# Convolution, attention and experts over 16 images: the next image's start inside the expert layer, combine weights by DMA, and the score tiles of a pair apart

## The chip, the cores and the metric

One core of a Trainium2 chip runs the whole program. The metric is the time on the device in microseconds (us), lower is better. The core has TensorE (PE, matmuls; PEld is its weight load), VectorE (DVE), ScalarE (ACT), GpSimd (POOL) and SyncE (SP, which issues the DMA transfers here). They run side by side and wait for each other through semaphores. Matmuls write into PSUM, which has 8 banks of 128 x 512 values.

## The reference

Sixteen images of 256 channels by 1024 pixels go through three layers. Cut to what is computed:

```
q, k, v = 1x1 convolutions of x to 32 channels
x = conv1x1(softmax(q @ k) @ v, Wo) * gamma + x          # 32 x 32 channel attention
t = tokens(x)                                            # 1024 tokens of 256
n = layernorm(t)
a1 = softmax(q1 @ k1 / s); a2 = softmax(q2 @ k2 / s)     # 8 heads of 32, over 1024 keys
o  = (a1 - lam * a2) @ v                                 # two softmaxes a head
t  = t + groupnorm(o) @ out_w.T + out_b
n = layernorm(t)
probs = softmax(n @ router); combine = the two largest of 8, else 0
y = shared(n) + sum over e of combine[:, e] * ((silu(n @ Wg[e]) * (n @ Wu[e])) @ Wd[e])
out = t + y
```

## The kernel before, in words

One loop over the 16 images ("batches"). The order of the work on every engine is written out by hand, and each engine keeps to it.

**Projection and first scores.** `layer_norm(0)` turns the normalised tokens back to channels. Four query and key projections follow (`proj`), written as three matmuls a product (a value split in a high and a low part, `split_mm`, L853). ACT takes the high part of each into `stage` (L385, L387), DVE the low part (L609), and SP copies both to `stack`. ACT waits for `y_out[1]`, the store of the image before, ahead of the first of these, since both use `stage`.

**Attention.** There are 16 units (8 heads, two softmaxes), each with 8 key tiles, taken as 4 pairs of tiles: 64 pairs. Of each key tile PE makes the transposed scores of 128 keys by 1024 queries as two matmuls (L1033, to PSUM banks 4 and 5, one half each), ACT takes the exponential of each half into `probs` (L411), and PE multiplies with the values (`weighted`, L985). A column of sums (`add_up`, L992) follows in three pairs of four. There is only one PSUM bank for each half, so the matmul of a tile's half waits until ACT has taken the same half of the tile before.

The maximum that the softmax subtracts is found 12 tiles ahead: PE makes the plain scores of 128 queries by 1024 keys (`score`, L964), DVE reduces them (L614). The eight columns of a unit are then turned by a transpose (`turn`, L970), which DVE takes out in a high and a low part (L623, L624) and SP puts into `stack`. Scores, turns and projections share a ring of two PSUM slots (four banks): item n waits for DVE to have freed item n - 2 (`ring_free`). `ring_order()` lists which items stand beside which pair (`BESIDE`): two scores a pair, the turn in pair 2 of a unit, and the four projections of the second head group in pairs (5, 1), (5, 2), (5, 3) and (6, 0). The last six pairs have no score beside them.

**Expert layer.** After the output projection (L1057) and the second layer norm come the router, its choice of two experts (a chain of small DVE steps, L768 to L786), and 18 steps (2 halves of the tokens, the shared expert and 8 experts). Step i on PE: gate and up (12 matmuls, L853), then a matmul (L1117) with a selecting column that spreads row e of the combine weights `comb_t` over all 128 partitions, then `down(i - 2)` (6 matmuls, L1087). `comb_t` is split in two parts by ACT (L463) and DVE (L805). On ACT: tanh (L470) and the high part of the hidden values (L455). On DVE: three products (L818, L826, L827; the last one with the spread weights out of PSUM), then the low part of the step before (L791). `down(i)` waits for the low part of step i.

**The next image.** Its convolution is spread over steps 9 to 11 (`conv_q`, `conv_scores`, `conv_wo`). `conv_last` (L897), the transposes to tokens (L917), the statistics and the normalisation stand behind the last step, between `down(15)` and the first projection, with `down(16)` and `down(17)` among them.

## Time and profile before

| | |
|---|---|
| median of 3 runs | 6543.28 us (6539.59 to 6547.5) |
| profiled execution | 6535.96 us, its span 6533.1 us |
| busy, share of the span | PE 93%, DVE 72%, ACT 47%, POOL 47% |
| granted TensorE clock, mean | 0.97 |
| chain that ended last, by engine | PE 82%, DVE 10%, ACT 3%, issue 3%, DMA 1% |
| one image | about 403 us |

The span is what lies between the first and the last instruction; the profiled execution's own time is 3 us above it. A clock of 1.00 is 2.4 GHz, one of 0.50 is 1.2 GHz. A busy time counts a matmul from its start to its end, though the next one starts before that: back to back, 512 columns start every 0.23 us. A start is therefore more use than a duration here.

### The profile page before, as it was taken

How to read it: one execution, taken by the hardware profiler on the slowest of the kernel's cores; microseconds unless marked ns; L12 is line 12 of the kernel's file. 1: busy time of each engine (PE TensorE's matmuls, PEld its weight loads, DVE VectorE, ACT ScalarE, POOL GpSimd, SP SyncE). 2: the span in 40 equal slices, each digit the busy share in tenths (PEclk: the TensorE clock that was granted, in tenths of full speed). 3: DMA queues.
4: the chain of work that ended last, by engine and by line, in shares of the span. 5: the costliest groups of instructions: out<-in, count | busy, mean ns of one | idle time of the engine just before them, and what ended most of it. 6: DMA issues, size and time to landing. Idle time of an engine off the chain costs nothing.

```text
span 6533.1 us, 125913 instructions
## 1 busy us (share of the span) xinstructions
PE 6063.3 (93%) x41498; PEld 3899.9 (60%) x41498; DVE 4700.7 (72%) x6535; ACT 3089.8 (47%) x5470; POOL 3092.9 (47%) x1382
## 2 busy tenths in 40 slices
PE   6999999899999999999999999999999999999998
PEld 4565565655656566565665656556565565655656
DVE  5767777676776767767677676776767767677676
ACT  4535445354453544535445354453544535355353
POOL 3706437074470734707347073471725617256271
PEclk9999999999999999999999999999999999999999
DMA  2202122121221212212022120221202212021120
GB/s 77 49 27 52 32 47 45 31 51 28 48 45 30 53 29 45 45 29 58 25 48 48 28 54 24 50 47 28 59 19 51 47 32 55 18 55 43 37 54 17
DMA packets 111217, 271.38 MB, mean 42 GB/s; under 512 B 34000, under 2 KB 56656, under 8 KB 102096
## 3 DMA queue, kind: packets, MB, share of 16 engines
q1 hardware_dynamic: 110544, 262.73, 17.4%
q8 instruction: 384, 6.29, 0.4%
q14 instruction: 289, 2.37, 0.1%
HBM read 23.38 MB, written 16.78 MB: 6 GB/s over the span
## 4 chain that ended last, share of the span: by engine, by line
PE 82%; DVE 10%; ACT 3%; issue 3%; DMA 1%; SPq 0%; DVEq 0%; ACTq 0%
PE psum L1033 19%; PE psum L853 17%; PE psum L985 15%; PE psum L964 14%; PE psum L1087 5%; PE psum L992 5%; DVE minus_max L614 2%; PE psum L1057 2%; PE psum L1012 1%; DVE small L550 1%; ACT probs L411 1%; PE psum L1117 1%; DVE max_rows L623 1%; DVE max_rows L624 1%; DMA stack<-stage 1%
## 5 line engine op out<-in xcount | busy, mean ns | idle before, releaser
L329 POOL TENSOR_TENSOR prob_sums<-probs 128x1024 f32<-128x1024 f32 x752 | 1795.2, 2387 | 3207.9 <-ACT probs L411 2923.4
L411 ACT ACTIVATE probs<-psum 128x512 f32<-128x512 f32 x4096 | 2222.9, 595 | 1419.9 <-PE psum L1033 1408.0
L614 DVE TENSOR_REDUCE minus_max<-psum 128x1 f32<-128x1024 f32 x2048 | 2422.4, 1209 | 398.6 <-PE psum L964 391.7
L1033 PE MATMUL psum<-stack 98*128 98x512 f32 x4096 | 1479.5, 438 | 43.9 <-ACT probs L411 41.7
L964 PE MATMUL psum<-stack 96*128 96x512 f32 x4096 | 1241.3, 412 | 106.0 <-DVE max_rows L624 64.9
L329 POOL TENSOR_TENSOR prob_sums<-prob_sums,probs 128x1024 f32<-128x1024 f32 x512 | 1220.2, 2383 | 101.5 <-ACT probs L411 62.6
L1033 PEld LDWEIGHTS psum<-stack 98*128 98x128 f32 x4096 | 704.9, 190 | 737.3 <-ACT probs L411 480.2
L985 PE MATMUL psum<-probs,v_tokens 128*32 128x256 f32 x16384 | 1112.2, 388 | 0.0
L964 PEld LDWEIGHTS psum<-stack 96*128 96x128 f32 x4096 | 721.5, 191 | 409.2 <-DVE max_rows L624 171.2
L853 PE MATMUL psum<-act_hi,w_hi 128*128 128x512 f32 x1728 | 713.7, 413 | 62.0 <-DVE minus_max L614 48.3
L985 PEld LDWEIGHTS psum<-probs,v_tokens 128*32 128x32 f32 x16384 | 429.4, 109 | 465.8 <-issue 288.9
L853 PE MATMUL psum<-act_lo,w_hi 128*128 128x512 f32 x1728 | 697.2, 403 | 0.0
L853 PE MATMUL psum<-act_hi,w_lo 128*128 128x512 f32 x1728 | 694.7, 402 | 0.0
L470 ACT ACTIVATE stage<-psum 128x512 f32<-128x512 f32 x288 | 172.6, 599 | 897.1 <-PE psum L1117 813.1
L635 DVE RECIPROCAL recip_sum<-psum 128x128 f32<-128x128 f32 x512 | 472.7, 931 | 118.7 <-PE psum L992 115.4
L818 DVE SCALAR_TENSOR_TENSOR stage<-stage,psum 128x512 f32<-128x512 f32 x288 | 197.6, 686 | 431.6 <-ACT stage L470 431.6
L992 PE MATMUL psum<-prob_sums,ones 128*32 128x256 f32 x6016 | 462.2, 379 | 0.0
L853 PEld LDWEIGHTS psum<-act_hi,w_hi 128*128 128x128 f32 x1728 | 334.8, 194 | 174.5 <-DVE minus_max L614 75.8
L1087 PE MATMUL psum<-stack,w_hi 128*128 128x512 f32 x1152 | 414.8, 401 | 6.0 <-DVE small L564 6.0
L853 PEld LDWEIGHTS psum<-act_lo,w_hi 128*128 128x128 f32 x1728 | 334.8, 194 | 78.1
L853 PEld LDWEIGHTS psum<-act_hi,w_lo 128*128 128x128 f32 x1728 | 335.7, 194 | 73.7
L992 PEld LDWEIGHTS psum<-prob_sums,ones 128*32 128x32 f32 x6016 | 195.6, 110 | 129.0
(141 smaller groups left out, 4744.7 us busy)
## 6 DMA issues: line engine op xcount, KB each, us to landing
stack<-stage SPq DMA_DIRECT2D x1024, 128.0 KB, 3.0
stack<-stage SPq DMA_DIRECT2D x256, 256.0 KB, 3.1
x_tile<-x_dram SPq DMA_DIRECT2D x17, 1024.0 KB, 4.8
x_tile<-o_head SPq DMA_DIRECT2D x512, 32.0 KB, 1.8
stack<-max_rows SPq DMA_DIRECT2D x512, 4.0 KB
y_dram<-residual SPq DMA_DIRECT2D x16, 512.0 KB, 2.8
y_dram<-stage SPq DMA_DIRECT2D x16, 512.0 KB, 3.7
stage<-w_split_dram SPq DMA_DIRECT2D x1, 3848.0 KB, 12.5
```

Source lines behind the costliest of these rows:

```text
L329: nc.gpsimd.tensor_tensor(total, first, probs[:, k % NP, :], ALU.add).then_inc(sum_pool, 1)
L411: nc.scalar.activation(probs[:, k % NP, half * HALF:(half + 1) * HALF], ps[:, 4 + half, :], ACT.Exp).then_inc(p_ready, 1)
L470: nc.scalar.activation(th[:, i % 2, :], ps[:, 2 + 3 * (i % 2), :], ACT.Tanh, scale=0.5).then_inc(f_th, 1)
L614: v.tensor_reduce(nm[:, u % 2, q:q + 1], flat_in, AX.X, ALU.max, negate=True).then_inc(ring_free, 1)
L635: v.reciprocal(rec[:, cols], ps[:, 6 + u % 2, CQ + cols.start:CQ + cols.stop]).then_inc(step, 1)
L818: link(v.scalar_tensor_tensor(gu, th[:, i % 2, :], 1.0, ps[:, bank, :], ALU.add, ALU.mult))
L853: ins = mm(dst, wt[:, w + kt * wn[0]:w + kt * wn[0] + wn[1]], xx[:, kt, act_cols], start=(first and n == 0), stop=(last and n == 3 * CT - 1))
L964: last = mm(slot[:, half, :], stack[0:AUX, s, 0, q * P:(q + 1) * P], stack[0:AUX, s, 1, half * HALF:(half + 1) * HALF], start=True, stop=True)
L985: last = mm(ps[HD * c:HD * c + HD, bank, 0:CQ], vt[:, kt, HD * h:HD * h + HD], probs[:, k % NP, c * CQ:(c + 1) * CQ], start=(kt == 0), sto ...
L992: ins = mm(ps[HD * c:HD * c + HD, 6 + u % 2, CQ:2 * CQ], ones[:, :], tile[:, c * CQ:(c + 1) * CQ], start=False, stop=last, skip_group_chec ...
L1033: mm(ps[:, 4 + half, :], stack[0:KS, s, 1, kt * P:(kt + 1) * P], stack[0:KS, s, 0, half * HALF:(half + 1) * HALF], start=True, stop=True). ...
L1087: last = mm(ps[:, t, :], wt[:, col:col + P], hx[:, i % 2, :], start=(e == 0 and n == 0), stop=(e == NE - 1 and n == 2))
```

## The change

Three parts, made together.

1. **The next image inside the expert layer.** `conv_q`, `conv_scores`, `conv_wo` move to steps 0, 1 and 3, `conv_last` to steps 4 and 5, the transposes to tokens to steps 6 and 8, statistics and normalisation to steps 7 to 13, half of the transposes back to step 12, the other half behind the gate and up of step 17. They use the two PSUM banks `SPARE = (4, 7)`; tokens are copied out of PSUM by ACT and normalised in place there. The sum goes to `x_tile` and is copied to `residual` later. The first half of projection 0 stands ahead of `down(17)`.
2. **Combine weights spread by transfers.** L1117 and the split of `comb_t` go. ACT copies the weights to SBUF, SP stores them in DRAM (32 KB) and, when that has landed, reads each expert's row back to all 128 partitions: 8 transfers of 256 KB a half, 16 an image. DVE's third product reads them from SBUF and waits for the transfer.
3. **The score tiles of a pair apart.** Of the two scores beside a pair one stays between the pair's two key tiles, the other one goes behind the pair's `weighted` and `add_up`, with the projection. The turn goes behind the second key tile. ACT does the projection's high part a pair later.

```
-                        for item in BESIDE.get((u, pair), []):      # DVE
+                        items = BESIDE[u, pair]
+                        for item in [it for it in items if it[0] == "turn" or it == items[0]]:
                             ring_step(item)
...
-                            if kt % 2 == 0:                          # PE
-                                for item in BESIDE[u, pair]:
+                            for item in BESIDE[u, pair][:1] if kt % 2 == 0 else []:
+                                if item[0] == "score":
                                     ring_step(item)
+                        for item in BESIDE[u, pair]:
+                            if item[0] == "turn":
+                                ring_step(item)
...
                         weighted(*divmod(k - 1, NT))
                         for late in ones_after(u, pair):
                             add_up(*late)
+                        for item in BESIDE[u, pair][1:]:
+                            if item[0] != "turn":
+                                ring_step(item)
...
-                        v.tensor_tensor(hid[:, i % 2, :], guu, ps[:, bank + 2, :], ALU.mult).then_inc(f_hid, 1)
-                    if i:
+                        dve.wait_ge(cb_in[e - 1], (b * NH + half + 1) * 16)
+                        v.tensor_tensor(hid[:, i % 2, :], guu, comb_bc[e - 1], ALU.mult).then_inc(f_hid, 1)
+                    if 0 < i < NH * NE - 1:
                         hidden_lo(i - 1)
...
+                for i in range(NH * E):                              # SP
+                    half, n = divmod(i, E)
+                    if half:
+                        sp.wait_ge(f_hid, b * NH * NE + n + 2)
+                    elif n == 0:
+                        sp.wait_ge(cb_row, b + 1)
+                        sp.dma_start(comb_rows, comb_t).then_inc(cb_out, 16)
+                        sp.wait_ge(cb_out, b * 16 + 16)
+                    sp.dma_start(comb_bc[n], comb_rows[n:n + 1, half * HALF:(half + 1) * HALF]
+                                 .broadcast_to([P, HALF])).then_inc(cb_in[n], 16)
...
-                    if e:                                            # PE, expert step i
-                        last = mm(ps[:, bank + 2, :], wh[:, W_SEL + e - 1:W_SEL + e].broadcast_to([P, P]), comb_t[:, cols],
-                                  start=True, stop=True)
-                    last.then_inc(f_full, 1)
...
+                        if i == 0 and part == 0:
+                            turn_logits()
+                            conv_q(b + 1)
+                    last.then_inc(f_full, 1)
                     if i == 1:
+                        conv_scores(b + 1)
...
+                    if i == 3:
                         conv_wo(b + 1)
-                    if i >= 2:
+                    if i in (4, 5):
+                        conv_last(b + 1, i - 4)
+                    if i in (TOKENS_AT, TOKENS_AT + 2):
+                        first_tokens(b + 1, i > TOKENS_AT)
+                    if i == TOKENS_AT + 6:
+                        first_back(b + 1, 0)
+                    if i == NH * NE - 1:
+                        first_back(b + 1, 1)
+                    if i >= 2 and i < NH * NE - 1:
                         down(i - 2)
-
+                down(NH * NE - 3)
+                down(NH * NE - 2)
                 pe.wait_ge(f_hid, b * NH * NE + NH * NE - 1)
-                for k in range(3):
-                    conv_last(k)
-                pe.wait_ge(f_hid, b * NH * NE + NH * NE)
-                conv_last(3)
-                tokens(b + 1, 0)
-                down(NH * NE - 2)
-
-                pe.wait_ge(t_var, b * 2 + 3)
+                first_projection(b + 1, 0)
                 down(NH * NE - 1)
```

In the next fences a row is one instruction, or several equal ones (x2), with its line and what it writes and reads; register and semaphore instructions stand among them.

PE inside attention, one plain pair before: the two halves of a key tile (L1033), four score matmuls (L964), the second key tile, the values (L985), the sums (L992).

```order
212 L1033 MATMUL psum<-stack 128x512
213 L1032 REGISTER_ALU
214 L1033 MATMUL psum<-stack 128x512
215 L948 REGISTER_ALU
216 L964 MATMUL psum<-stack 128x512 x2
217 L948 REGISTER_ALU
218 L964 MATMUL psum<-stack 128x512 x2
219 L1032 REGISTER_ALU
220 L1033 MATMUL psum<-stack 128x512
221 L1032 REGISTER_ALU
222 L1033 MATMUL psum<-stack 128x512
223 L985 MATMUL psum<-probs,v_tokens 32x256 x8
```

PE at a like place now (L1185 is the key tile, L1116 the score, L1137 the values, L1144 the sums):

```order
178 L1116 MATMUL psum<-stack 128x512 x2
179 L1184 REGISTER_ALU
180 L1185 MATMUL psum<-stack 128x512
181 L1184 REGISTER_ALU
182 L1185 MATMUL psum<-stack 128x512
183 L1098 REGISTER_ALU
184 L1116 MATMUL psum<-stack 128x512 x2
185 L1184 REGISTER_ALU
186 L1185 MATMUL psum<-stack 128x512
187 L1184 REGISTER_ALU
188 L1185 MATMUL psum<-stack 128x512
189 L1137 MATMUL psum<-probs,v_tokens 32x256 x8
```

Two score matmuls stand between the key tiles, where four stood; the other two stand ahead of the pair.

PE at the end of the expert layer before, behind `down(15)`: the last convolution, the transposes to tokens, then the last two `down`.

```order
1561 L1125 REGISTER_ALU
1562 L897 MATMUL psum<-stage 128x512 x3
1563 L1128 REGISTER_ALU
1564 L897 MATMUL psum<-stage 128x512
1565 L915 ISA
1566 L917 MATMUL psum<-w_full,residual 128x128 x8
1567 L915 REGISTER_ALU
1568 L917 MATMUL psum<-w_full,residual 128x128 x8
1569 L1087 MATMUL psum<-stack,w_hi 128x512
```

PE there now, between the gate and up of step 17 and `down(15)` (L1246):

```order
1548 L1039 REGISTER_ALU
1549 L1042 ISA
1550 L1045 MATMUL psum<-w_full,stage 128x128 x4
1551 L1042 REGISTER_ALU
1552 L1045 MATMUL psum<-w_full,stage 128x128 x4
1553 L1246 MATMUL psum<-stack,w_hi 128x512
```

Only the second half of the transposes back is left there. DVE in steps 1 and 2 now (L935, L943 and L945 are the three products, L898 the low part of the step before):

```order
588 L935 SCALAR_TENSOR_TENSOR probs<-probs,psum 128x512
589 L619 REGISTER_ALU
590 L943 TENSOR_TENSOR probs<-probs,psum 128x512
591 L619 REGISTER_ALU
592 L944 REGISTER_ALU
593 L945 TENSOR_TENSOR probs<-probs,prob_sums 128x512
594 L898 TENSOR_TENSOR stack<-probs,stack 128x512
```

The wait for the transfer stands at 592, and the low part that `down(0)` needs (594) behind it.

## Rows read from the trace of the kernel before

**Rows 1.** Who waited for whom on PE: us in total, times, longest

```profile
PE psum L964 <- DVE max_rows L624: 64.9, 213, 0.4
PE psum L853 <- DVE minus_max L614: 48.3, 64, 0.9
```

**Rows 2.** Timeline of PE, a plain pair: start, us, then idle before

```profile
2221.97 0.84 PE L1033 MATMUL psum<-stack 98*128 98x512 f32 x2
2222.66 1.09 PE L964 MATMUL psum<-stack 96*128 96x512 f32 x4
2223.58 0.63 PE L1033 MATMUL psum<-stack 98*128 98x512 f32 x2
2224.14 1.07 PE L985 MATMUL psum<-probs,v_tokens 128*32 128x256 f32 x16
...
2225.57 0.50 PE L1033 MATMUL psum<-stack 98*128 98x512 f32 x1
```

**Rows 3.** Timeline of ACT, the exponentials of the second key tile of that pair

```profile
2224.01 1.08 ACT L411 ACTIVATE probs<-psum 128x512 f32<-128x512 f32 x2 [0.42 <-PE psum L1033]
```

**Rows 4.** Timeline of PE, a pair of the last unit, with no score beside it

```profile
2346.97 0.73 PE L1033 MATMUL psum<-stack 98*128 98x512 f32 x2
2348.15 0.99 PE L1033 MATMUL psum<-stack 98*128 98x512 f32 x2 [0.45 <-ACT probs L411]
2349.07 1.07 PE L985 MATMUL psum<-probs,v_tokens 128*32 128x256 f32 x16
...
2350.50 0.50 PE L1033 MATMUL psum<-stack 98*128 98x512 f32 x1
```

**Rows 5.** Timeline of PE, start of the pair behind a turn pair

```profile
2229.76 0.50 PE L1033 MATMUL psum<-stack 98*128 98x512 f32 x1
```

**Rows 6.** Groups of instructions: taking a projection out of PSUM, a hidden product, busy and mean ns

```profile
L609 DVE SCALAR_TENSOR_TENSOR stage<-psum,w_full,stage 128x1024 fp32r<-128x1024 f32 x64 | 82.1, 1284 | 136.8 <-ACT stage L387 136.8
L387 ACT ACTIVATE stage<-psum,w_full 128x1024 fp32r<-128x1024 f32 x64 | 71.3, 1115 | 200.6 <-PE psum L853 200.6
L827 DVE TENSOR_TENSOR stage<-stage,psum 128x512 f32<-128x512 f32 x256 | 175.7, 686 | 8.9
```

**Rows 7.** One image in stretches: us, then PE, PEld, DVE, ACT, POOL busy, PEclk, DMA

```profile
2388.68:2410.68 22.00, 18.34 (x80) 14.33 (x80) 13.59 (x31) 6.16 (x10) 0.00 (x0) 0.92 0.02 5
2410.68:2470.87 60.19, 60.02 (x273) 47.71 (x272) 36.44 (x59) 14.88 (x28) 0.00 (x0) 1.00 0.03 10
2470.87:2485.80 14.93, 14.64 (x56) 10.18 (x54) 12.68 (x31) 4.07 (x7) 0.00 (x0) 0.89 0.00 1
2485.80:2504.76 18.96, 15.15 (x66) 11.75 (x65) 8.63 (x13) 7.66 (x11) 0.00 (x0) 0.91 0.32 80
2519.07:2762.84 243.77, 233.49 (x1921) 133.07 (x1919) 187.00 (x211) 141.71 (x258) 191.30 (x86) 0.99 0.22 48
```

**Rows 8.** The same for attention of the image before

```profile
2113.00:2359.37 246.37, 236.11 (x1921) 133.93 (x1919) 187.19 (x211) 141.70 (x258) 191.33 (x86) 0.98 0.21 47
```

**Rows 9.** Timeline of all engines, the logits' turn, then the combine weights

```profile
2390.17 0.33 PE L1071 MATMUL psum<-w_full,stage 128*128 128x128 f32 x1 [1.32 <-DVE stage L765]
...
2397.68 1.01 ACT L463 ACTIVATE stack<-psum 8x1024 fp32r<-8x1024 f32 x1 [3.05 <-PE psum L1110]
...
2399.99 0.50 PE L1117 MATMUL psum<-stack,w_hi 128*128 128x512 f32 x1 [2.35 <-DVE stack L805]
```

**Rows 10.** Timeline of PE: the last convolution; 16 transposes to tokens at full clock

```profile
2069.59 3.74 PE L897 MATMUL psum<-stage 32*128 32x512 f32 x8
...
2375.93 2.10 PE L917 MATMUL psum<-w_full,residual 128*128 128x128 f32 x16
```

**Rows 11.** DMA issues: KB each, median us from issue to landing

```profile
stack<-stage SPq DMA_DIRECT2D x1024, 128.0 KB, 3.0
...
x_tile<-o_head SPq DMA_DIRECT2D x512, 32.0 KB, 1.8
...
y_dram<-stage SPq DMA_DIRECT2D x16, 512.0 KB, 3.7
```

More of the change, by code:

```diff
@@ L96, in ring_order @@
         for pair in range(PAIRS):
-            beside[u, pair] = [("turn", u + 1)] if 2 * pair == 2 * NT - AHEAD and u + 1 < UNITS else []
-            for kt in (2 * pair, 2 * pair + 1):
-                n = u * NT + kt + AHEAD
-                if n < UNITS * NT:
-                    beside[u, pair].append(("score", *divmod(n, NT)))
-            if (u, pair) in PROJ_BESIDE:
-                beside[u, pair].append(("proj", 4 + PROJ_BESIDE.index((u, pair))))
+            scores = [("score", *divmod(n, NT)) for n in range(u * NT + 2 * pair + AHEAD, u * NT + 2 * pair + AHEAD + 2)
+                      if n < UNITS * NT]
+            turn = [("turn", u + 1)] if 2 * pair == 2 * NT - AHEAD and u + 1 < UNITS else []
+            proj = [("proj", 4 + PROJ_BESIDE.index((u, pair)))] if (u, pair) in PROJ_BESIDE else []
+            beside[u, pair] = scores[:1] + turn + scores[1:] + proj
     return before, beside
@@ L367, in normalise, with copy_tokens, token_deviation @@
                     last.then_inc(n_act, 1)
-            normalise(0, 0)
+            def copy_tokens(n, half):
+                for k in range(2):
+                    act.wait_ge(l_stat, n * 4 + 2 * half + k + 1)
+                    nc.scalar.activation(xt[:, 4 * half + 2 * k:4 * half + 2 * k + 2, :],
+                                         ps[:, SPARE[k], :].rearrange("p (t c) -> p t c", t=2),
+                                         ACT.Copy).then_inc(l_copied, 1)
+            def token_deviation(n):
+                act.wait_ge(t_var, n * 2 + 1)
+                nc.scalar.activation(small[:, 64:72], small[:, 56:64], ACT.Sqrt).then_inc(t_sd, 1)
@@ new lines, in normalise_tokens, with take_high @@
+            def normalise_tokens(n, half):
+                act.wait_ge(t_rs, n * 2 + 1)
+                act.wait_ge(l_copied, n * 4 + 4)
+                for tt in range(4 * half, 4 * half + 4):
+                    last = nc.scalar.activation(xt[:, tt, :], xt[:, tt, :], ACT.Identity,
+                                                bias=small[:, 80 + tt:81 + tt], scale=small[:, 72 + tt:73 + tt])
+                last.then_inc(l_norm, 1)
+            def take_high(n, half):
+                for k in range(2):
+                    act.wait_ge(back_full, n * 8 + 2 * half + k + 1)
+                    nc.scalar.activation(xh[:, k, half * HALF:(half + 1) * HALF], ps[:, SPARE[k], :],
+                                         ACT.Copy).then_inc(back_hi, 1)
@@ new lines, in keep_residual @@
+            def keep_residual(n, t):
+                act.wait_ge(x_used, n * 4 + 4)
+                nc.scalar.activation(res[:, t, :], xin[:, t, :], ACT.Copy).then_inc(res_in, 1)
+            for t in range(CT):
+                keep_residual(0, t)
+            for half in range(NH):
+                copy_tokens(0, half)
+            token_deviation(0)
+            for half in range(NH):
+                normalise_tokens(0, half)
+            for half in range(NH):
+                take_high(0, half)
@@ L543, in link_from, with token_statistics, statistics @@
                 dve.wait_ge(step, base + taken[0])
-            def statistics(n, i, base):
+            def token_statistics(n, half):
+                for k in range(2):
+                    dve.wait_ge(t_full, n * 8 + 2 * half + k + 1)
+                    for q in range(2):
+                        tt = 4 * half + 2 * k + q
+                        ins = v.bn_stats(small[:, 112 + 6 * tt:118 + 6 * tt], ps[:, SPARE[k], q * C:(q + 1) * C])
+                        if q == 0:
+                            ins.then_inc(step, 1)
+                            taken[0] += 1
+                    ins.then_inc(l_stat, 1)
+            def statistics(n, base):
                 for k in range(4):
-                    dve.wait_ge(t_full, n * 8 + 4 * i + k + 1)
+                    dve.wait_ge(t_full, n * 8 + 4 + k + 1)
                     for tt in (2 * k, 2 * k + 1):
@@ L905, in _, with tokens @@
             conv_wo(0)
-            pe.wait_ge(a2_ready, 1)
-            for k in range(4):
-                conv_last(k)
-            def tokens(n, i):
+            for half in range(NH):
+                conv_last(0, half)
+            for half in range(NH):
+                first_tokens(0, half)
+            for half in range(NH):
+                first_back(0, half)
+            first_projection(0, 0)
+            def tokens(n):
                 for tt in range(NT):
                     if tt % 4 == 0:
-                        pe.wait_ge((x_used, y1_ready)[i], n * 4 + tt // 2 + 2)
+                        pe.wait_ge(y1_ready, n * 4 + tt // 2 + 2)
                     for ct in range(CT):
```

301 lines of the change are left out of this document (185 added, 116 removed).

## The prediction, made before the changed kernel ran

> **What bounds the kernel now.** I began with who waits for whom on PE, since PE is busy nearly always, then read the timeline of PE and ACT inside attention, where most of an image's time lies, and last the image in stretches. In the first view the waits that part 3 of the change is about are small: PE waits 64.9 us in all for the turned maxima and 48.3 us for the slot of a projection [rows 1]. The timeline shows a plain pair of key tiles from its first matmul at 2221.97 to the next pair's at 2225.57: 3.60 us, and no idle time is noted in it [rows 2]. So a plain pair is paid by PE alone; a new order can't make it shorter, only add waits. Its neighbour with the turn runs from 2225.57 to 2229.76, 4.19 us [rows 2, 5]. One image is, in the stretches [rows 7]: router end to gate and up of step 4, 22.00 us; from there to step 17, 60.19; to the end of the last down product, 14.93; to the first score, 18.96; attention from its first to its last key tile, 243.77 us (246.37 the image before, at a clock of 0.98 for 0.99 [rows 8]).
>
> **Attention: why the score between the tiles matters.** A half of a key tile can't be started before ACT has taken the same half of the tile before, since each half has one bank. In the plain pair four score matmuls cover that: the first tile starts at 2221.97, the second 1.61 us later. How long ACT needs is read at two places. Behind a warm start the exponentials begin 0.43 us after the matmul (2223.58 to 2224.01) and both halves take 1.08 us [rows 2, 3]; so the second half is free 1.51 us after the tile's start, and the second tile's second half could start at about 1.56. The other place is a pair with no score beside it: there the second tile starts 1.18 us after the first with a wait for ACT (2346.97 to 2348.15, 0.45 us idle), its two halves take 0.99 us in place of 0.63, and the values follow 0.92 us behind instead of 0.56 [rows 2, 4]. Four matmuls start within 0.92 us, 0.23 each (2222.66 to 2223.58 [rows 2]). The scoreless pair has so much less to do on PE and yet takes 3.53 us, 2346.97 to 2350.50 [rows 4]: ACT's answer sets it.
>
> After the change two of the four score matmuls are left between the tiles, so PE comes to the second tile at 0.93 us and to its second half at 1.16, against about 1.08 and 1.56 when ACT lets it go. The values then start 0.44 behind (cold) and not 0.33: 2.00 us after the pair's start, where 1.49 would be the cost without a wait. The wait costs 0.5 us. Counted from the other side: the scoreless pair's 3.53 us covers the score that stays (it fits into the idle 0.45 us), and the score that went behind the sums adds its own 0.46, which makes 3.99. The plain pair of the rows takes 3.60, of which its slow first tile is 0.11 (0.84 for 0.73 [rows 2, 4]): 3.49 to 3.60 before, 0.39 to 0.50 more now. I take **0.48 us a plain pair**. Bounds: 0.15 if only the first half's wait told, 0.6 if the cold restart costs at each half.
>
> Of 64 pairs, 58 have scores; 14 of them have the turn, 4 a projection (one has both), and 41 are plain: 41 x 0.48 = 19.7 us an image. In a **turn pair** the turn stands behind the second tile, by when its last maximum is ready, since PE waits for ACT there anyway; the wait of 0.3 us for its result goes (64.9 us over 213 times [rows 1]), the wait for ACT comes: 4.3 us for 4.19, 13 x 0.1 = 1.3. In the **projection pairs** the wait for a maximum goes (48.3 us over 64 times, 0.75 each [rows 1]). But ACT now takes the projection behind the next pair's exponentials: about 1.5 + 1.1 + 1.3 = 3.9 us after its end [rows 3, 6]. The second score of that pair needs the slot at 3.4, 0.5 us too early; in the pair with the turn the turn needs it at 1.6, 2.4 us too early; and DVE's reduction of the next score stands behind it, 0.8 us for the last two projections. The four pairs and the one behind them come out at 2.2 us more, and I add 0.8 for a fall of the clock: 3.0. Attention in all: 19.7 + 1.3 + 3.0 = **24.0 us an image, 384 us for 16**.
>
> **The expert layer.** *Start.* What goes: the wait for the copied logits, 1.3 us (gate and up cover it), and that for the split of the weights, 2.35 [rows 9]. What comes is a chain: the transposes of the weights, now behind `conv_q` and `conv_scores`, are done at about 2397.9 on the old clock; ACT's copy 1.0 us [rows 9]; a store of 32 KB to DRAM and a load of 256 KB. No row has either; each lies between 1.8 us (32 KB on the chip) and 3.7 (512 KB to DRAM) [rows 11]. I take 2.1 for the store, near the 32 KB, and 3.0 for the load, the value of 128 KB. DVE's third product of step 1 then starts at 2404.4. Behind it stands the low part of step 0, which `down(0)` waits for: 2405.9 (two operations of 0.7 [rows 6]), and PE is there at 2400.8. So 5.1 us of new wait (3.6 to 7.4), 16 times. The stretch, with one fall of the clock as before: 22.0 - 0.7 (three spreading matmuls) + 2.3 (moved convolution, below) - 1.3 - 2.35 + 5.1 = 25.1, **+3.1**. The other 15 transfers have a step of 4.2 us each for their landing and cost nothing; if they landed later than a step each, every step would wait for them.
>
> The Trainium skill ("DMA: Bandwidth & Descriptors", part "Anatomy of one DMA") gives about 2.0 us plus the bytes at 436 GB/s for a transfer. By that the two would be 2.1 and 2.6 us, an estimate, and the wait 0.4 shorter than the one taken, 6 us over the run; no row of the kernel before shows these transfers.
>
> *Middle.* The 13 steps of 19 matmuls at 0.23 (0.2315) make 57.2 of the 60.19 us [rows 7]; most of the other 3.0, I take 2.3, are `conv_q`, `conv_scores` and `conv_wo`. The spreading matmul goes: -3.0. In come `conv_last` 3.74 us, 16 transposes 2.10, eight more at half of that, 1.0 [rows 10]; the three small pieces, 2.3, leave. `down(9)` waits for the sum of the first half on DVE, which has lost 1.3 us of cover: 0.8. DVE has 1.4 us free in each step (2.75 of 4.16: four operations at 0.69 [rows 6]), and each inserted piece is about that long. Sum: -3.0 + 6.8 - 2.3 + 0.8 = +2.3; I take **+2.2**.
>
> *End.* From step 17 to the last down product: gate and up 2.8, transposes back 1.0, three down products 4.2, half a projection 1.4, all covered for DVE and ACT: 9.4 for 14.93: **-5.6**.
>
> *Boundary.* The other half of the projection and the second one take to 4.4 us after the last down. Then ACT must wait for `y_out[1]`: the sum of the second half on DVE at 1.5 (two operations [rows 6]), the store 3.7 us [rows 11], so ACT starts at 5.3; its copy and DVE's low part, 2.3 [rows 6], free the slot at 7.8. PE waits 3.4 us there, a wait that the old order hid. Two projections follow, and the copies to `stack` (3.0 [rows 11]) land at the same time: first score at 13.4, with a fall of the clock 14.7, for 18.96: **-4.3**.
>
> **The sum.** 16 x (3.1 + 2.2 - 5.6) + 15 x (-4.3) = -69; the first image's serial start +4: -65 us for parts 1 and 2. Attention +384. The profiled execution takes 6535.96 us: 6535.96 - 65 + 384 = 6855. It stands 7 us below the median of the runs shown, so **6860 us**, 4.9% slower.
>
> **Rivals.** *A, the wait doesn't come (the one on the other side).* The exponentials might be taken before PE comes to the second tile, so that the plain pair stays as long as it is and the waits of the first view go: 6543 - 65 - 64.9 - 48.3 = 6365. It decides at 178 / (16 x 41) = 0.27 us a plain pair; below that, with those waits gone, the change is faster. For it speaks that only 0.15 us are missing for the first half; against it the second half, and the scoreless pair, in which PE demonstrably waits [rows 4]. *B, half of it.* PE loses 0.25 a plain pair, because the pipeline refills as in a warm start: 41 x 0.25 x 16 = 164, the turn and projection pairs 69, so 6543 - 65 + 233 = 6711. *C, the clock.* More idle pieces in every pair let the clock fall inside attention. The image with a mean clock of 0.98 over 246 us took 2.6 us longer than the one with 0.99 [rows 7, 8]; each further 0.04 would cost some 10 us an image, 160 in all: 7020. Against it: nothing in the scoreless pairs, whose waits are as long, points to it, as their matmuls keep full pace (1.07 us for the values [rows 4]). *D, the transfers are late.* If a load took over 4.2 us each, the steps would go by them, 16 x 1 us an image: 7120.
>
> The Trainium skill names such a case ("TensorE: Matmul & The Clock Gate", part "A second HAM failure mode: psum-queue depth-cycling"): short idle times between groups of matmuls make the clock go up and down. By that rule the time would be C's. The rows here speak against it: full pace beside such waits [rows 4].
>
> **How the numbers follow.** Forecast 0.70, B 0.10, C 0.07, D 0.03, A 0.10. The range 6680 to 6960 leaves out A, C, D (0.20) and holds the forecast with 0.35 to 0.6 us a pair, a first load that lands 2 us later or 1.5 sooner, and B. A measurement of this kernel tells about 0.2%, 13 us, from no change. Faster by more: 0.10; within: 0.02; slower: 0.88.
>
> **What would show it.** On PE, the wait of the second key tile for ACT should grow to some 200 to 300 us over all, and a plain pair to 4.0 us; the wait for the turned maxima should be nearly gone. `down(0)` waits about 5 us for DVE, and projection 2 about 3.4 us. No matmul spreads weights, step 5 takes no more than 4.2 us and its own moved work. The forecast is wrong if plain pairs stay under 3.7 us, or if attention grows by more than 30 us an image.

## The result, and the profile after

The changed kernel takes 6853.5 us (median of 4 runs, 6836.9 to 6869.35) against 6542.74 us for the kernel before on the same chip: ratio 1.0474, 95% interval 1.0454 to 1.0494. It is 4.7% slower, 6.5 us below the forecast of 6860. The profiled execution takes 6844.29 us with a span of 6842.4.

Inside attention, the PE timeline of a plain pair after the change (start, us, then idle before; L1185 key tile, L1116 scores, L1137 values, L1144 sums):

```profile
3501.62 0.73 PE L1116 MATMUL psum<-stack 96*128 96x512 f32 x2
3502.19 0.63 PE L1185 MATMUL psum<-stack 98*128 98x512 f32 x2
3502.66 0.63 PE L1116 MATMUL psum<-stack 96*128 96x512 f32 x2
3503.27 0.98 PE L1185 MATMUL psum<-stack 98*128 98x512 f32 x2
3504.19 1.07 PE L1137 MATMUL psum<-probs,v_tokens 128*32 128x256 f32 x16
3505.07 0.61 PE L1144 MATMUL psum<-prob_sums,ones 128*32 128x256 f32 x8
3505.62 0.73 PE L1116 MATMUL psum<-stack 96*128 96x512 f32 x2
```

From the score at 3501.62 to the like score at 3505.62 a pair takes 4.00 us, against 3.53 us before in most pairs (3.60 in [rows 2]). The second key tile starts 1.08 us after the first (3502.19 to 3503.27), though only two score matmuls of 0.23 us stand between. The values start 0.92 us behind it. Before, four matmuls stood there, and the values followed 0.56 us behind [rows 2]. The 0.92 is that of the scoreless pair, in which PE waited for ACT [rows 4]: now each plain pair looks like it. And the wait has no bracket here (a bracket notes idle time and what ended it): no idle time is noted. ACT in the same pair:

```profile
3502.62 2.27 ACT L470 ACTIVATE probs<-psum 128x512 f32<-128x512 f32 x4 [1.29 <-PE psum L1185]
```

ACT takes the four halves in one run of 2.27 us and starts 0.43 us after PE. In [rows 3] it stood idle for 0.42 us between the two tiles of a pair; now PE brings the second tile before ACT is free.

The groups of instructions, before (L1033, L411) and after. Columns: busy us, mean ns of one, then idle time ahead and what ended it:

```profile
L1033 PE MATMUL psum<-stack 98*128 98x512 f32 x4096 | 1479.5, 438 | 43.9 <-ACT probs L411 41.7
...
L1033 PEld LDWEIGHTS psum<-stack 98*128 98x128 f32 x4096 | 704.9, 190 | 737.3 <-ACT probs L411 480.2 <-issue 196.2
```

```profile
L1185 PE MATMUL psum<-stack 98*128 98x512 f32 x4096 | 1676.9, 454 | 43.4 <-ACT probs L470 43.4
...
L1185 PEld LDWEIGHTS psum<-stack 98*128 98x128 f32 x4096 | 774.1, 191 | 891.1 <-ACT probs L470 775.2 <-issue 26.3
```

The same 4096 matmuls keep PE "busy" for 197 us more, and its weight load waits 295 us more for ACT (775.2 for 480.2), while PE's own idle time behind ACT hardly moves (43.4 us for 41.7). In these pairs the wait is shown as the length of the matmuls and as idle time of the weight load.

Who waited for whom, after (us in total, times, longest us):

```profile
PE psum L1246 <- DVE stack L898: 77.9, 16, 5.1
...
PE psum L1116 <- DVE stage L715: 43.4, 63, 1.3
PE psum L971 <- DVE stage L715: 40.6, 15, 2.9
```

The wait for the turned maxima, 64.9 us in [rows 1], is gone from the list. `down(0)` (L1246) waits 4.9 us each time for the low part, projection 2 (L971) 2.7 us for its slot, and a new one stands between the first score and the first key tile: a score (L1116) waits for the slot of projection 3.

One image in the stretches of [rows 7]: router end to gate and up of step 4, to step 17, to the last down product, to the first score, to the first key tile (which has no row there), to the last key tile. Columns as in [rows 7]:

```profile
3358.30:3383.90 25.60, 20.53 (x103) 15.51 (x102) 13.82 (x35) 6.57 (x12) 0.00 (x0) 0.87 0.35 108
3383.90:3445.80 61.90, 61.22 (x267) 47.53 (x266) 42.41 (x76) 26.13 (x46) 0.00 (x0) 1.00 0.10 35
3445.80:3455.00 9.20, 9.20 (x45) 7.40 (x43) 6.79 (x11) 2.84 (x5) 0.00 (x0) 1.00 0.02 6
3455.00:3472.10 17.10, 13.48 (x44) 10.21 (x44) 4.93 (x5) 4.34 (x4) 0.00 (x0) 0.80 0.31 80
3472.10:3487.80 15.70, 12.77 (x75) 10.25 (x74) 13.97 (x14) 3.51 (x5) 0.00 (x0) 1.00 0.48 101
3487.80:3752.00 264.20, 256.43 (x1921) 135.62 (x1919) 188.59 (x211) 141.34 (x258) 191.06 (x86) 0.99 0.20 44
```

Its boundary is not the usual one: no other has two falls of the clock (0.80 here, 0.90 in most). The medians over all images, worked out from the start of each instruction, beside the forecast:

| stretch, us an image | before | after | change | forecast |
|---|---|---|---|---|
| expert start | 22.0 | 25.5 | +3.5 | +3.1 |
| middle | 60.2 | 61.9 | +1.7 | +2.2 |
| end | 15.0 | 9.2 | -5.8 | -5.6 |
| boundary | 18.5 | 16.4 | -2.1 | -4.3 |
| first score to first key tile | 14.4 | 16.2 | +1.8 | 0 |
| attention (sum of the medians of its pairs) | 243.4 | 263.7 | +20.3 | +24.0 |

They add up to +19.4, times 16 = 310 us; the spans differ by 309.3.

### The profile page after: what moved, and what is told of

It reads as the page before. It is cut to its first block, busy times and chain, and to the rows that moved or that the text cites. A ratio compares the mean times of both kernels' runs of the same rounds, so it can differ in the third digit from the quotient of the medians.

```text
span 6842.4 us, 126541 instructions
## 1 busy us (share of the span) xinstructions
PE 6359.5 (93%) x41264; PEld 3874.4 (57%) x41264; DVE 4672.8 (68%) x6455; ACT 3204.1 (47%) x5660; POOL 3087.7 (45%) x1382
## 4 chain that ended last, share of the span: by engine, by line
PE 83%; DVE 6%; ACT 4%; issue 3%; DMA 2%; POOL 1%; ACTq 0%; DVEq 0%; SPq 0%; POOLq 0%
PE psum L1185 20%; PE psum L971 16%; PE psum L1116 16%; PE psum L1137 14%; PE psum L1246 6%; PE psum L1144 4%; PE psum L1215 2%; ACT probs L470 1%; DVE stage L715 1%; DVE minus_max L720 1%; PE psum L1164 1%; PE psum L1020 1%; DMA y_dram<-stage 1%; DMA prob_sums<-combine_rows_dram 1%; ACT stage L446 1%
## 5 line engine op out<-in xcount | busy, mean ns | idle before, releaser
L470 ACT ACTIVATE probs<-psum 128x512 f32<-128x512 f32 x4096 | 2225.2, 595 | 2049.5 <-PE psum L1185 1816.1
L1185 PE MATMUL psum<-stack 98*128 98x512 f32 x4096 | 1676.9, 454 | 43.4 <-ACT probs L470 43.4
L1116 PE MATMUL psum<-stack 96*128 96x512 f32 x4096 | 1420.6, 429 | 57.6 <-DVE stage L715 43.4
L1185 PEld LDWEIGHTS psum<-stack 98*128 98x128 f32 x4096 | 774.1, 191 | 891.1 <-ACT probs L470 775.2
L1137 PE MATMUL psum<-probs,v_tokens 128*32 128x256 f32 x16384 | 1114.4, 388 | 0.0
L1116 PEld LDWEIGHTS psum<-stack 96*128 96x128 f32 x4096 | 696.8, 192 | 570.3 <-issue 325.0
L971 PE MATMUL psum<-act_hi,w_hi 128*128 128x512 f32 x1730 | 711.9, 412 | 108.2 <-DVE stage L715 40.6
L971 PE MATMUL psum<-act_lo,w_hi 128*128 128x512 f32 x1730 | 698.6, 404 | 0.0
L971 PE MATMUL psum<-act_hi,w_lo 128*128 128x512 f32 x1730 | 698.0, 403 | 0.0
L1137 PEld LDWEIGHTS psum<-probs,v_tokens 128*32 128x32 f32 x16384 | 429.9, 110 | 438.3 <-issue 259.6
L524 ACT ACTIVATE probs<-psum 128x512 f32<-128x512 f32 x288 | 172.2, 598 | 764.7 <-PE psum L971 764.7
L1246 PE MATMUL psum<-stack,w_hi 128*128 128x512 f32 x1152 | 432.5, 419 | 88.8 <-DVE stack L898 77.9
L1144 PE MATMUL psum<-prob_sums,ones 128*32 128x256 f32 x6016 | 463.2, 380 | 0.0
L971 PEld LDWEIGHTS psum<-act_hi,w_hi 128*128 128x128 f32 x1730 | 336.8, 195 | 220.2 <-DVE stage L715 47.3
L935 DVE SCALAR_TENSOR_TENSOR probs<-probs,psum 128x512 f32<-128x512 f32 x288 | 197.5, 686 | 372.8 <-ACT probs L524 370.7
L971 PEld LDWEIGHTS psum<-act_lo,w_hi 128*128 128x128 f32 x1730 | 336.5, 194 | 78.3
L971 PEld LDWEIGHTS psum<-act_hi,w_lo 128*128 128x128 f32 x1730 | 336.5, 194 | 76.4
L1246 PEld LDWEIGHTS psum<-stack,w_hi 128*128 128x128 f32 x1152 | 224.8, 195 | 177.5 <-issue 131.4
```

Of the source, the lines that this page charges most:

```text
L470: nc.scalar.activation(probs[:, k % NP, half * HALF:(half + 1) * HALF], ps[:, 4 + half, :], ACT.Exp).then_inc(p_ready, 1)
L524: nc.scalar.activation(th[:, i % 2, :], ps[:, 2 + 3 * (i % 2), :], ACT.Tanh, scale=0.5).then_inc(f_th, 1)
L935: link(v.scalar_tensor_tensor(gu, th[:, i % 2, :], 1.0, ps[:, bank, :], ALU.add, ALU.mult))
L971: ins = mm(dst, wt[:, w + kt * wn[0]:w + kt * wn[0] + wn[1]], xx[:, kt, act_cols], start=(first and n == 0), stop=(last and n == 3 * CT - 1))
L1116: last = mm(slot[:, half, :], stack[0:AUX, s, 0, q * P:(q + 1) * P], stack[0:AUX, s, 1, half * HALF:(half + 1) * HALF], start=True, stop=True)
L1137: last = mm(ps[HD * c:HD * c + HD, bank, 0:CQ], vt[:, kt, HD * h:HD * h + HD], probs[:, k % NP, c * CQ:(c + 1) * CQ], start=(kt == 0), sto ...
```

## Experiments

My theory was that parts 1 and 2 gain about 1% at most, and that the loss is ACT's answer in each plain pair. The rivals: the clock, ring waits on DVE, or contention from the new transfers. Ratios are to the kernel before on the same chip, with 95% intervals.

### Part 3 alone, and parts 1 and 2 alone

The first run has only the attention part of the diff, the second all but that. Parts 1 and 2 were not run apart from each other, so the share of each is not shown.

> The kernel before with the third part of the change alone: one of a pair's two scores behind the sums, the turn behind the second key tile, the projection with it. My theory (the second key tile has to wait for ACT's exponentials, and this alone makes the loss): attention grows by about 21 us an image as in the changed kernel, 16 x 21 = 336, so 6543 + 336 = 6880 us (6850 to 6905), plain pair 4.0 us. Rival (the loss comes from the parts acting together, the expert layer's moved work and transfers having a share of it): below 6800 us.

> The changed kernel with attention's order as before (both scores and the projection between the key tiles, turn first), the next image inside the expert layer and the weights spread by transfers kept. My theory: 6853 - 336 = 6517 us (6500 to 6535), attention back at 244 to 246 us an image, slightly faster than the kernel before; the plain pair 3.53 us. Rival (the two parts act together): over 6600 us. Second rival (the expert layer's part gains nothing): 6543 or above.

Part 3 alone: 6860.32 us, ratio 1.0493 (1.0475 to 1.051). Parts 1 and 2 alone: 6521.97 us, 0.9973 (0.9962 to 0.9985). Together they give 1.0466 against the 1.0474 of the full change. So part 3 is the whole loss. It is as large in a kernel that has none of the new transfers, so their contention isn't its cause. Its key tile row (L1033 here) reads like that of the full change:

```profile
L1033 PE MATMUL psum<-stack 98*128 98x512 f32 x4096 | 1671.2, 453 | 43.4 <-ACT probs L412 43.4
```

The mean clock of that run is 0.971, that of the kernel before 0.97: the clock isn't the cause either. Inside attention, PE's clock was at the lower level for 108 us in all before and 120 us after the change, summed over the 16 images; the 12 us more are far too little for the 325 us by which attention grew.

### A short exponential

ACT takes the exponential of 128 of the 512 columns of each half (the other values are a constant 1), so that it answers sooner; PE's work and order are those of the changed kernel.

```
-  nc.scalar.activation(probs[:, k % NP, half * HALF:(half + 1) * HALF], ps[:, 4 + half, :], ACT.Exp)
+  nc.scalar.activation(probs[:, k % NP, half * HALF:half * HALF + P], ps[:, 4 + half, 0:P], ACT.Exp)
```

> The changed kernel with the exponential taken of the first 128 of each half's 512 columns only (the other columns of the probabilities are left out and hold a constant), all orders and waits kept. Theory (PE waits for ACT): an exponential of 0.3 us in place of 0.6 frees both banks before PE comes, the plain pair falls from 4.01 to about 3.50, the turn pairs and the scoreless pairs lose 0.5 and 0.9: 16 x (21 + 6.5 + 5) = 520 us less, 6330 us (6280 to 6420). Rival (the loss is in PE's own restarts or in the ring and DVE, whatever ACT does): 6750 us or more.

6374.25 us, ratio 0.9747 (0.973 to 0.9763). PE and ACT in a plain pair:

```profile
4446.01 0.74 PE L1117 MATMUL psum<-stack 96*128 96x512 f32 x2
4446.59 0.63 PE L1186 MATMUL psum<-stack 98*128 98x512 f32 x2
4447.06 0.63 PE L1117 MATMUL psum<-stack 96*128 96x512 f32 x2
4447.53 0.63 PE L1186 MATMUL psum<-stack 98*128 98x512 f32 x2
4448.09 1.07 PE L1138 MATMUL psum<-probs,v_tokens 128*32 128x256 f32 x16
```

```profile
4447.03 0.51 ACT L470 ACTIVATE probs<-psum 128x128 f32<-128x128 f32 x2 [1.63 <-PE psum L1186]
```

With the exponentials of two halves at 0.51 instead of some 1.1 us, the second key tile starts 0.94 us after the first, which is when PE gets there; the values follow 0.56 behind, and a plain pair takes 3.49 to 3.50 us in the median. In the pairs without a score the wait is gone too: 2.96 us for 3.54. The new order costs PE nothing by itself; the 0.5 us a pair are the wait for ACT.

### Three of the four score matmuls between the tiles

In the full change, the first half of the second score goes back between the key tiles, to give PE another 0.23 us of cover.

```
-  for item in BESIDE[u, pair][:1] if kt % 2 == 0 else []:
+  for item in BESIDE[u, pair] if kt % 2 == 0 else []:
       if item[0] == "score":
-          ring_step(item)
+          second = item != BESIDE[u, pair][0]
+          if not second:
+              ring_step(item)
+          elif len(BESIDE[u, pair]) == 2:
+              ring_step(item, (0,))                 # first half only
 ...
-  ring_step(item)                                   # behind the sums
+  ring_step(item, (1,) if len(BESIDE[u, pair]) == 2 else (0, 1))
```

> The changed kernel with three of the four score matmuls of a plain pair between the key tiles, in place of two: the second score's first half stays there, its second half stands behind the sums. Theory (only the time until ACT lets go of the bank counts): the second tile's first half no longer waits, its second half waits until the same 1.56 us, so the plain pair takes 3.77 us for 4.01: 41 x 0.24 x 16 = 157 us less, 6853 - 157 = 6696 us (6670 to 6730). Rival 1 (the price is for interrupting, or for the maxima's tiles being apart, and not for the wait): no change, 6853 us. Rival 2 (only the first half's wait matters): back to about 6540 us.

I was wrong in sign: 6998.21 us, ratio 1.07 (1.0682 to 1.0718). The waits of PE, then the last pair of a unit, which has no sums:

```profile
PE psum L1116 <- DVE minus_max L720: 249.0, 653, 0.5
```

```profile
5300.25 0.63 PE L1187 MATMUL psum<-stack 98*128 98x512 f32 x2
5300.72 0.63 PE L1116 MATMUL psum<-stack 96*128 96x512 f32 x2
5301.73 0.50 PE L1116 MATMUL psum<-stack 96*128 96x512 f32 x1 [0.38 <-DVE minus_max L720]
5302.07 0.63 PE L1187 MATMUL psum<-stack 98*128 98x512 f32 x2
```

The third matmul belongs to the next item of the ring. It waits until DVE has reduced the score of two items before, which comes, in part or whole, only at the end of the pair before. So PE idles 0.38 us and comes to the second tile 1.82 us after the first. In the median such a pair takes 3.72 us for 3.57 in the changed kernel, a plain one 4.15 for 4.01. This run doesn't test how much cover ACT needs, since the ring's wait came in its place. It does show a second limit: two slots and a reduction of 1.2 us set how close two scores may stand.

### The turn late, alone

On parts 1 and 2 alone, both scores stay between the tiles, and the turn moves behind the second tile.

```
-  ring_step(item)                       # PE, between the key tiles
+  if item[0] != "turn":
+      ring_step(item)
+  for item in BESIDE[u, pair]:          # PE, behind the second key tile
+      if item[0] == "turn":
+          ring_step(item)
```

The ring's order goes with it, from turn, score, score to score, score, turn.

> As e2, but with the turn behind the second key tile, while both scores stay between the tiles; DVE takes the turn right behind the second score. Theory (the wait for the turned maxima costs 0.3 to 0.4 us a turn pair and the late turn is free of it): turn pair 3.8 us for 4.2, 14 x 0.35 x 16 = 78 us less than e2, 6440 us. Rival (the turned rows reach the stack too late for the next unit, so PE waits at the unit's start, 0.5 to 1.5 us each): no gain or up to 200 us slower than e2.

Another miss: 6568.03 us, ratio 1.004 (1.0025 to 1.0056). PE in a turn pair, from its second key tile (L1189) to the turn (L1126):

```profile
5375.39 0.68 PE L1189 MATMUL psum<-stack 98*128 98x512 f32 x2
5376.41 0.27 PE L1126 MATMUL psum<-w_full,minus_max 128*8 128x128 f32 x1 [0.35 <-DVE minus_max L721]
```

The turn is ready by its own data, but its slot in the ring is that of the pair's first score, which DVE is still reducing: 80.6 us over 224 turns, more than the 64.9 us that went. In the median the pair takes 4.15 us (about 4.2 before), pair 0 of a unit 3.66 to 3.73 for 3.54, and the pair (5, 3) 9.79 for 7.28. The late turn gives its own pair 0.05 us at most, and other pairs pay more than that.

### ACT's wait for the store, moved

On parts 1 and 2 alone, ACT waits for `y_out[1]` only ahead of projection 3, the first that overwrites what the store reads.

```
-  act.wait_ge(y_out[1], b * 16 + 16)
 ...
+  if t == 3:
+      act.wait_ge(y_out[1], b * 16 + 16)
```

> As e2 (attention as before), but ACT waits for the store of the image before only ahead of projection 3, the one whose place in the stage the store still reads, and not ahead of projection 0. Theory (the store sets the start of the projections now): PE's wait before projection 2, 2.7 to 2.9 us in 15 images, goes, and up to 1 us of the wait behind it: 45 us less than e2 (30 to 65). Rival (the transfers of the stack for the first score are next and end it at the same time): less than 15 us.

6445.9 us, ratio 0.9855 (0.9836 to 0.9874): 76 us or 1.2% less than parts 1 and 2 alone, more than expected. What the wait cost is seen in the changed kernel. ACT, then PE at the boundary (last down product at 3454.81):

```profile
3461.20 1.28 ACT L444 ACT_TABLE_LOAD   x1 [8.97 <-DMA y_dram<-stage]
```

```profile
3454.81 0.40 PE L1246 MATMUL psum<-stack,w_hi 128*128 128x512 f32 x1
3457.01 0.49 PE L971 MATMUL psum<-act_hi,w_hi 128*128 128x512 f32 x1 [1.80 <-issue]
...
3458.60 0.63 PE L971 MATMUL psum<-act_hi,w_hi 128*128 128x512 f32 x1
3459.03 0.63 PE L971 MATMUL psum<-act_hi,w_lo 128*128 128x512 f32 x1
...
3464.83 0.51 PE L971 MATMUL psum<-act_hi,w_hi 128*128 128x512 f32 x1 [1.82 <-DVE stage L715]
```

Three things add up. ACT goes on only when the store has landed, here 6.2 us after the end of the last down product (5.6 us in the median of the 15 boundaries). The load of its function table, 1.28 us, stands behind the same wait; with the wait moved it runs beside the last down products. And PE idles twice, 1.80 and 1.82 us, and behind each idle piece matmuls start every 0.43 us (3458.60 to 3459.03) instead of 0.23, for some 3 us: the lower clock level, 1.2 GHz. Two such falls make this image an exception. Of the other 14 boundaries 13 have one, behind the second idle piece (2.6 to 2.9 us), and a granted clock of about 0.90; one has none. With the wait moved, only one of 15 has a fall there. One image of that run, in the stretches from the last down product to the first score and on to the first key tile:

```profile
5244.90:5258.00 13.10, 10.34 (x44) 7.67 (x43) 5.12 (x6) 4.69 (x5) 0.00 (x0) 1.00 0.44 114
5258.00:5272.30 14.30, 12.72 (x74) 10.34 (x75) 13.90 (x14) 2.39 (x4) 0.00 (x0) 0.99 0.49 102
```

In the medians the boundary takes 13.5 us for 16.4, and first score to first key tile 14.5 for 16.2.

### The low part ahead of the wait for the row

On parts 1 and 2 alone, DVE makes the low part of step 0 before it waits for the first row of weights.

```
+  if i == 1:
+      hidden_lo(0)
   dve.wait_ge(cb_in[e - 1], ...)
   v.tensor_tensor(hid[:, i % 2, :], guu, comb_bc[e - 1], ALU.mult)
-  if 0 < i < NH * NE - 1:
+  if 1 < i < NH * NE - 1:
       hidden_lo(i - 1)
```

> As e2, but in step 1 DVE makes the low part of step 0 before it waits for the first transferred row, and not behind it. Theory (down(0) waits 4.9 us because it stands behind that wait on DVE; then the next gate and up waits for step 1's product instead, which comes when the row lands): 1.4 us an image come free, the time of down(0), 20 us less than e2 (12 to 30). Rival (nothing is gained since the row's landing sets step 3 in any case): 0 to 8 us.

6470.71 us, ratio 0.9895 (0.9878 to 0.9911), again more than expected. The wait of `down(0)` is gone, and PE waits once later:

```profile
PE psum L973 <- DVE probs L947: 44.2, 16, 2.9
```

That is 2.8 us each for 4.9. The start of the expert layer falls from 25.5 to 22.1 us in the median, more than the 2.1 us of wait. Two images of this run show why:

```profile
4371.60:4393.30 21.70, 18.64 (x103) 13.93 (x102) 14.22 (x36) 6.54 (x12) 0.00 (x0) 1.00 0.38 115
3971.90:3996.10 24.20, 21.36 (x104) 15.80 (x102) 14.35 (x36) 6.54 (x12) 0.00 (x0) 0.86 0.40 115
```

The same work takes 21.7 us at a granted clock of 1.00 and 24.2 at 0.86. In the changed kernel, behind the idle piece of 5 us, all 16 images fall and take 25.4 us or more (clock 0.87 in the one shown above); with 2.8 us 8 of 16 stay at 1.00. So a wait here costs itself and up to 2.5 us of clock.

### Both mends, and the rows without DRAM

The first has the last two edits together, on parts 1 and 2 alone. The second is the first, but reads each row of weights from its own SBUF partition:

```
-  sp.dma_start(comb_rows, comb_t).then_inc(cb_out, 16)          # store to DRAM, and a wait for it
-  sp.dma_start(comb_bc[n], comb_rows[n:n + 1, cols].broadcast_to([P, HALF]))
+  row = comb_t[n:n + 1, cols]                                   # one SBUF partition
+  sp.dma_start(comb_bc[n].rearrange("p (o n) -> p o n", o=1), row.unsqueeze(1).broadcast_to([1, P, HALF]))
```

> The expert-layer part alone, with both mends: ScalarE waits for the store of the output tile only ahead of projection 3, and VectorE does the low part of step 0 ahead of its wait for the weight row. They lie at different places of an image (boundary, start), so theory: their gains add, ratio 0.9973 - 0.0118 - 0.0078 = 0.978, about 6395 us (6375 to 6420); start of the expert layer about 22 to 24 us, boundary about 13.4 us. Rival: part of the gain of each was the same granted clock, so that both together give no more than the larger, about 6440 us.

> As the run with both mends, but each row of weights is spread to the partitions by a transfer that reads it from its own SBUF partition, with no store to DRAM ahead of it. Theory: the store and its landing (about 2.3 us) leave the chain from router to the first row, and the wait of step 3 for it (5.3 us a time with the store, 2.9 us more for the second in line) shrinks by as much: 16 times 2.3 us = 37 us, about 6360 us (6345 to 6390). Rival: 128 reads of one partition are slower than the same bytes from DRAM (over 6 us instead of 3.7 to 4.2 us from issue to landing); then the step waits longer than before and the time is 6420 us or more.

Both mends: 6405.58 us, ratio 0.9794 (0.978 to 0.9807), so the gains add nearly in full, and this version beats both kernels. One image of it, from the router's end to the last key tile:

```profile
2350.10:2371.50 21.40, 18.59 (x103) 13.92 (x102) 14.19 (x36) 6.55 (x12) 0.00 (x0) 1.00 0.35 114
2371.50:2433.40 61.90, 61.22 (x267) 47.52 (x266) 42.25 (x75) 26.06 (x45) 0.00 (x0) 1.00 0.11 40
2433.40:2442.60 9.20, 9.20 (x45) 7.40 (x43) 6.80 (x11) 3.59 (x6) 0.00 (x0) 1.00 0.01 4
2442.60:2456.30 13.70, 10.52 (x44) 7.68 (x43) 5.10 (x6) 4.82 (x5) 0.00 (x0) 1.00 0.43 109
2456.30:2470.50 14.20, 12.61 (x73) 10.28 (x74) 13.80 (x14) 2.39 (x4) 0.00 (x0) 1.00 0.50 103
2470.50:2712.80 242.30, 232.04 (x1922) 131.92 (x1921) 187.05 (x211) 141.73 (x259) 191.37 (x86) 1.00 0.22 48
```

In this image every stretch is at full clock, and PE is 96 to 100% busy in the middle, the end and attention; start and boundary still hold idle time. It is a good image: in 13 of the 16 the clock is at its lower level for 3 to 10 us around the start of attention, as it is in 10 images of the kernel before and in 12 of the changed one, and the median attention takes 245.4 us. None of the edits here goes at that.

Without DRAM it is the rival that holds, by far: 7702.98 us, ratio 1.1773 (1.1757 to 1.1789). The DMA issues (KB each, median us from issue to landing), first of the changed kernel, then of this one:

```profile
prob_sums<-combine_rows_dram SPq DMA_DIRECT2D x128, 256.0 KB, 3.7
stage<-combine_rows_dram SPq DMA_DIRECT2D x128, 256.0 KB, 4.2
```

```profile
prob_sums<-probs SPq DMA_DIRECT2D x128, 256.0 KB, 30.8
stage<-probs SPq DMA_DIRECT2D x128, 256.0 KB, 30.8
```

This time runs from issue to landing and holds the waiting behind transfers issued before. DVE's product with the first three rows of one image, in the run without DRAM:

```profile
2785.87 0.69 DVE L946 TENSOR_TENSOR probs<-probs,prob_sums 128x512 f32<-128x512 f32 x1 [10.71 <-DMA prob_sums<-probs]
2795.79 0.69 DVE L946 TENSOR_TENSOR probs<-probs,prob_sums 128x512 f32<-128x512 f32 x1 [7.71 <-DMA prob_sums<-probs]
2805.54 0.69 DVE L946 TENSOR_TENSOR probs<-probs,prob_sums 128x512 f32<-128x512 f32 x1 [6.76 <-DMA prob_sums<-probs]
```

The first row was issued at 2773.88 and lands 12.0 us later, the next ones some 9.8 us apart: 256 KB in 9.8 us are 27 GB/s. In the changed kernel the first row of an image lands in 3.1 to 3.5 us and the seven behind it 0.7 to 1.1 us apart; a load with none before it in the queue takes 3.0 to 3.4. It is not that fewer DMA engines work: from 2773.9 to 2785.8 they are 83% busy and move 25 GB/s, from 3370.5 to 3374.0 in the changed kernel 58% busy at 180 GB/s. Why one source partition is so slow, no run here shows. The way over DRAM is the quick one. The middle stretch goes from 61.9 to 126.8 us in the median: rival D's mechanism (each step goes by its transfer), which the changed kernel doesn't reach.

## Why the prediction was right

**The plain pair was right, in mechanism and size.** 0.48 us forecast, 3.53 to 4.00 or 4.01 measured, in pairs without the sums 3.10 to 3.57. The step that carried it was the comparison with the scoreless pair [rows 4]: one look at a pair in which PE already waits for ACT gave the price of every other pair once its cover is gone. The short exponential shows the cause. Rivals A and B (0 and 0.25 us a pair) are out, and C too: the clock inside attention is 0.98 to 1.00 before and 0.97 to 1.00 after, image by image. Its falls lie at the start of attention and beside the projections, in both kernels.

**Attention as a whole was 3.7 us an image too dear.** Three terms of the sum were mis-sized. There are 38 plain pairs, not 41: I counted (0, 0), (0, 1), which hardly changed (they take 4.6 to 4.9 us in both kernels, most of them at the lower clock), and the one behind the projections among them, 1.4 us. The 13 turn pairs got 0.06 us cheaper each (4.12 for about 4.18), not 0.1 dearer: 2.1 us. The projection pairs and the one behind came to +3.3 for +3.0: (5, 1) shorter, 6.78 for 7.40, the four behind it longer (8.76, 8.74, 8.10 and 4.47 for 7.61, 7.28, 7.66 and 3.60).

**The boundary was 4 us an image too cheap, which hid the other.** Forecast -4.3; measured -2.1 and +1.8 behind it. The step that failed is the chain "store, ACT's copy, DVE's low part". In the median of the 15 boundaries the slot of the first projection was free 9.1 us after the end of the last down product and not 7.8: the table load of 1.28 us behind the wait was left out of the sum. The store came 0.3 late (5.6 for 5.3); the copy and the low part took the 2.3. The one fall of the clock that was counted is there in 13 of 15, and the first score comes at 16.4 for 14.7. The sum also ended at the first score, while the late chain of ACT and DVE still holds a score 1.35 us later, and in 11 of 16 images the clock falls again some 2 us ahead of the first key tile, which makes that stretch 16.16 us for 15.71: 1.8 us in all that no term had. The wait of projection 2 itself was smaller than forecast (2.7 us for 3.4), since PE idled some 1.6 us ahead of the second half of projection 0, which was left out too, and so came later; that lengthens nothing by itself. Both errors are about 60 us over the run, of opposite sign, and this is why 6860 came so near; the forecast was good to some 60 us a term, not to 7.

**Expert start, middle, end: right within 0.5 us.** `down(0)` waits 4.9 us for 5.1. The load, of which no row existed, landed in 3.7 to 4.2 us for 3.0 (medians, which hold the waiting behind the loads before it); in the image shown the store and its landing took 1.8 us for 2.1 (issue of the store at 3368.68, of the first load at 3370.49) and the first load 3.5, 5.3 us in all for 5.1, a load that was too cheap and a store that was too dear by as much. DVE's product there:

```profile
3373.99 0.69 DVE L945 TENSOR_TENSOR probs<-probs,prob_sums 128x512 f32<-128x512 f32 x1 [5.29 <-DMA prob_sums<-combine_rows_dram]
```

The Trainium skill ("DMA: Bandwidth & Descriptors", part "Anatomy of one DMA") gives 2.6 us for 256 KB, an estimate from its fit, which it states for transfers on GpSimd's path; these go by SP's queue. The measured loads take 1.1 to 1.6 us more in the median, those with none before them in the queue 0.4 to 0.8, and the measurement decides.

**One sign that I named was wrong.** PE's wait for ACT did not grow to 200 to 300 us in the view of waits: it went from 41.7 to 43.4. The growth is in the weight load's wait (+295 us) and in the length of the matmuls (+197 us). Whoever had looked at that one row would have called the theory false.

**The expectations of two experiments fell for one reason.** Late turn and three matmuls between were both costed against ACT and the data, and not against the ring: an item waits for the one two places ahead of it, so moving one item moves the wait of the next. What stays open is how ACT's answer would pay out with three matmuls between if the ring had a free slot; PSUM has none, and it wasn't tried.

## What to carry to other kernels

Work that stands between two uses of one buffer is cover, even if no wait is noted there: before moving it away, find a place in the trace where it is missing and read what that place costs. After moving a wait or adding a transfer, look at what stands behind the wait on the same engine (a table load, a low part that others need) and move it ahead; here these two edits turned a gain of 0.3% into 2.1%. Price every moved item against the ring or pool that it draws from too, not only against its data.

## What the runs showed of the hardware

- A transfer that spreads one row of 512 values to 128 partitions (256 KB) takes 3.0 to 3.5 us from DRAM if none stands before it in the queue, and 12.0 us from a single SBUF partition; in a row they land 0.7 to 1.1 and 9.8 us apart.
- Behind an idle piece of 1.8 to 5 us on PE, matmuls started every 0.43 us instead of 0.23 for some 3 to 4 us in many images, not in all (8 of 16 behind the one of 2.8 us in the run with the low part first). Waits of half a microsecond in each 4 us pair did not bring the clock down: in 264 us of attention it was at 0.99. The Trainium skill ("TensorE: Matmul & The Clock Gate", part "A second HAM failure mode: psum-queue depth-cycling") tells of a kernel in which short idle times between groups of matmuls made it go up and down; the plain pairs here don't show that.
- A matmul that waits for PSUM can be noted as a longer matmul (1676.9 for 1479.5 us of the same 4096), with the idle time on its weight load.
